# Rows of Wo freed of their mean, and the output projection of an attention layer spread over three slots

## The reference, cut to what matters

```python
x = x + _layernorm(_L0_attn_ref(_layernorm(x), Wqvk, Wo))     # x: (8, 1024, 512) f32
x = x + _layernorm(_L0_ffn_ref(_layernorm(x), W1, b1, ..., W2, b2))

def _layernorm(x, axis=-1, eps=1e-05):
    m = jnp.mean(x, axis=axis, keepdims=True)
    v = jnp.var(x, axis=axis, keepdims=True)
    return (x - m) / jnp.sqrt(v + eps)

def _L0_attn_ref(h, Wqvk, Wo):            # 16 heads of 32, causal
    ...
    wv = jnp.einsum('bsth,bthi->bshi', weights, v).reshape(b, s, d)
    return wv @ Wo
```

## Time and profile before

| | |
|---|---|
| median of three runs | 3590.53 us |
| profiled execution, whole | 3584.82 us |
| its span, first to last instruction | 3582.9 us |
| mean granted clock of TensorE | 0.956 of full |
| TensorE busy, matmuls | 3246.1 us (91%) |
| VectorE, ScalarE, POOL busy | 2240.6, 2105.8, 1333.6 us |

### The profile page before, as it was taken

How to read it: one execution, slowest core, us unless ns; L and a number is a source line. 1 busy time by engine, 2 the same in 40 slices (tenths; PEclk the granted TensorE clock), 3 DMA queues, 4 the chain that set the end, 5 groups by cost and what they waited for, 6 DMA issues and landing times. The chain is left out here.

```text
span 3582.9 us, 78215 instructions
## 1 busy us (share of the span) xinstructions
PE 3246.1 (91%) x29997; PEld 1878.0 (52%) x29997; DVE 2240.6 (63%) x4221; ACT 2105.8 (59%) x2516; POOL 1333.6 (37%) x766
## 2 busy tenths in 40 slices
PE   6999996989888889889898845999999999999998
PEld 2444442666666666667676722444444444444443
DVE  5444444777676777667676536666666666666665
ACT  2222221988888887979797924445445445445543
POOL 0000001888888897979797920000000000000000
PEclk9999996999999999999999967999999999999999
DMA  3344324122222222222213031000000000000000
GB/s 128 116 134 136 129 102 113 51 66 73 62 85 62 76 70 77 58 85 60 81 56 90 28 111 52 24 24 24 24 23 23 23 23 23 23 23 23 24 24 24
DMA packets 183098, 219.97 MB, mean 61 GB/s; under 512 B 15184, under 2 KB 129936, under 8 KB 182288
## 3 DMA queue, kind: packets, MB, share of 16 engines
q1 hardware_dynamic: 182800, 215.83, 19.1%
HBM read 130.84 MB, written 84.41 MB: 60 GB/s over the span
## 5 line engine op out<-in xcount | busy, mean ns | idle before, releaser
L949 POOL TENSOR_TENSOR a_prob_lo<-a_prob,a_prob_hi 128x2048 f16<-128x2048 f32 (+2 forms) x448 | 1192.1, 2689 | 249.9 <-ACT a_prob_hi L840 247.9
L870 DVE TENSOR_REDUCE a_mx<-a_pw 128x1 f32<-128x512 f32 (+3 forms) x1216 | 753.3, 657 | 165.7 <-PE a_pw L717 122.4
L830 ACT ACTIVATE a_prob<-a_pst,a_lift,a_exp_scale 128x1024 f32<-128x1024 f32 (+1 forms) x640 | 707.3, 1121 | 185.1 <-PE a_pst L770 97.6
L1387 PE MATMUL f_py<-f_w,f_act 128*128 128x512 f16 x3072 | 706.6, 380 | 20.2 <-DVE f_work L1153 12.8
L1377 PE MATMUL f_ph<-f_xT,f_w 128*128 128x512 f16 x3072 | 707.3, 380 | 0.0
L840 ACT ACTIVATE a_prob_hi<-a_prob 128x2048 f16<-128x2048 f32 (+2 forms) x448 | 582.7, 1301 | 0.0
L1325 ACT ACTIVATE f_hidden_work<-f_ph,f_turn,f_fold 128x512 f32<-128x512 f32 x256 | 199.0, 777 | 596.4 <-PE f_ph L1377 595.7
L712 PE MATMUL a_pw<-a_kp,a_qp 96*128 96x512 f16 (+3 forms) x1536 | 469.6, 342 | 75.0 <-DVE a_mx L870 58.4
L1108 POOL TENSOR_TENSOR f_ve<-f_mv,f_eps 128x4 f32<-128x4 f32 x32 | 9.0, 282 | 1384.5 <-DVE f_mv L1134 1384.5
L792 PE MATMUL a_acc<-a_vt,a_prob_hi 128*128 128x33 f16 x9216 | 468.4, 179 | 44.7 <-POOL a_prob_lo L949 24.4
L792 PEld LDWEIGHTS a_acc<-a_vt,a_prob_hi 128*128 128x128 f16 x9216 | 435.9, 97 | 125.3 <-DVE a_o L889 27.9
(11 more groups left out here) (170 smaller groups left out, 3526.0 us busy)
## 6 DMA issues: line engine op xcount, KB each, us to landing
qk_parts<-q_stage SPq DMA_DIRECT2D x128, 256.0 KB, 2.1
a_qp<-qk_parts SPq DMA_DIRECT2D x192, 128.0 KB, 2.6
a_kp<-qk_parts SPq DMA_DIRECT2D x192, 128.0 KB, 2.8
v_parts<-q_vstage SPq DMA_DIRECT2D x16, 1056.0 KB, 5.1
a_vt<-v_parts SPq DMA_DIRECT2D x32, 528.0 KB, 4.4
q_x<-in_L_attn_h_dram SPq DMA_DIRECT2D x16, 1024.0 KB, 7.7
a_xr<-in_L_attn_h_dram SPq DMA_DIRECT2D x64, 256.0 KB, 2.9
x<-a_y SPq DMA_DIRECT2D x64, 256.0 KB, 2.1
```

The costliest lines, as they stand in the source:

```text
L830: act.activation(prob[:, k % PR, :, off:QC], pst[:, k % 2, :, off:QC], ACT.Exp, scale=exp_scale[:, :], bias=lift[:, :]).then_inc(exp_done, 1)
L870: dve.tensor_reduce(out, src, AX_X, ALU.max).then_inc(released, 1)
L949: pool.tensor_tensor(prob_lo[:, first % HR:first % HR + steps, :, off:QC], prob[:, first % PR:first % PR + steps, :, off:QC], prob_hi[:, f ...
L1387: last = pe.matmul(py[:, t, :], act_r[:, f % AR, b, t * P:(t + 1) * P], w2s[:, a, f, :], start=(f == 0 and j == 0), stop=(f == NF - 1 and ...
```

## The change

Once, in the setup, VectorE takes the mean of each of Wo's 512 rows and subtracts it. Each row of wv @ Wo then has mean zero, its variance is what it was, and x + layernorm becomes one operation, pwo*rstd + x. ScalarE's shift and POOL's third small operation are gone. The scale is found from the subtracted rows. A tile's twelve matmuls stand in three slots, four in each. The statistics move to the end of slot 3, behind that slot's reduces, and POOL's two small operations to slot 3; y stays at the end of slot 4, in front of the statistics if two tiles met there.

```diff
-WO_STATS, WO_SMALL, WO_NORM, WO_OUT, WO_STORE = 2, 2, 3, 4, 5
+WO_PARTS = 3
+WO_STATS, WO_SMALL, WO_OUT, WO_STORE = 3, 3, 4, 5
...
                 for k in range(KT):
                     dve.wait_ge(w_loaded[k], 16)
-                    then(dve.tensor_reduce(amax[:, k:k + 1], raw[:, k, :], AX_X, ALU.max, apply_absolute_value=True))
+                    last = dve.tensor_reduce(row_mean[:, k:k + 1], raw[:, k, :], AX_X, ALU.add)
+                then(last)
+                then(dve.tensor_scalar(row_mean[:, :], row_mean[:, :], 1 / D, None, ALU.mult))
+                for k in range(KT):
+                    last = dve.tensor_scalar(raw[:, k, :], raw[:, k, :], row_mean[:, k:k + 1], None, ALU.subtract)
+                then(last)
+                for k in range(KT):
+                    last = dve.tensor_reduce(amax[:, k:k + 1], raw[:, k, :], AX_X, ALU.max, apply_absolute_value=True)
+                then(last)
...
-                    for w, a in PASSES:
-                        last = pe.matmul(pwo[:, :], oT[:, a, g, t * P:(t + 1) * P], wo[:, w, g, :],
-                                         start=(g == 0 and (w, a) == PASSES[0]),
-                                         stop=(g == GROUPS - 1 and (w, a) == PASSES[-1]))
-                    if g == GROUPS - 1:
+                    terms = [(g, a, w) for g in range(GROUPS) for w, a in PASSES]
+                    per = len(terms) // WO_PARTS
+                    for j, (g, a, w) in list(enumerate(terms))[part * per:(part + 1) * per]:
+                        last = pe.matmul(pwo[:, :], oT[:, a, g, t * P:(t + 1) * P], wo[:, w, g, :], start=(j == 0),
+                                         stop=(j == len(terms) - 1))
+                    if part == WO_PARTS - 1:
                         last.then_inc(wo_done, 1)
...
-                        for b, t in stage.tiles(u, k, WO_NORM):
-                            shift_x(i + b, t)
...
                 def wo_out(i, t):
                     s, n = t % YR, QT * i + t
-                    dve.wait_ge(x_shifted, n + 1)
+                    dve.wait_ge(small_done, 2 * n + 2)
+                    dve.wait_ge(xr_loaded[t % 2], 16 * (QT // 2 * i + t // 2 + 1))
                     wait(dve, y_stored[s], 16 * (QT // YR * i + t // YR))
                     dve.scalar_tensor_tensor(y[:, s, :], pwo[:, :], small[:, s, 1:2], xr[:, t % 2, :], ALU.mult,
-                                             ALU.subtract
+                                             ALU.add
                                              ).then_inc(y_done, 1)
...
                     for u, k in stage.slots:
-                        for b, t in stage.tiles(u, k, WO_STATS):
-                            wo_stats(i + b, t)
                         for at, what, unit, m in stage.at(u, k):
                             shared(i, at, before, what, unit, m, stage)
...
                         for b, t in stage.tiles(u, k, WO_OUT):
                             wo_out(i + b, t)
+                        for b, t in stage.tiles(u, k, WO_STATS):
+                            wo_stats(i + b, t)
...
-                    pool.wait_ge(small_done, 3 * n + 2)
-                    pool.tensor_tensor(small[:, s, 2:3], mv[:, s, 0:1], small[:, s, 1:2], ALU.mult
-                                       ).then_inc(small_done, 1)
```

More of the change, by code:

```diff
@@ L488, in attention_phase @@
         amax = sb("amax", [P, KT])
+        row_mean = sb("row_mean", [P, KT])
         top, o_pow2, o_scale, exp_scale = (sb(n, [P, 1]) for n in ("top", "o_pow2", "o_scale", "exp_scale"))
@@ L509, in attention_phase @@
         mv = sb("mv", [P, YR, 2])
-        small = sb("small", [P, YR, 3])
+        small = sb("small", [P, YR, 2])
         half = sb("half", [P, 1])
@@ L532, in attention_phase @@
         xr_loaded = [sem(f"xr_loaded{b}") for b in range(2)]
-        wo_done, x_shifted, y_done = sem("wo_done"), sem("x_shifted"), sem("y_done")
+        wo_done, y_done = sem("wo_done"), sem("y_done")
         y_stored = [sem(f"y_stored{b}") for b in range(YR)]
@@ L574, in _ @@
                 pe.wait_ge(const, 9)
-                pe.wait_ge(vec_step, KT + 1)
+                pe.wait_ge(vec_step, 5)
                 pe.transpose(pw[0:1, 0, 0:P], top[:, :], ident[:, :]).then_inc(top_turned, 1)
-                pe.wait_ge(vec_step, KT + 2)
+                pe.wait_ge(vec_step, 6)
                 pe.matmul(pw[:, 1, 0:2], ones[:, :], top_row[:, :].to_broadcast([1, 2]), start=True, stop=True
@@ L611, in _ @@
             def _(act):
-                act.wait_ge(vec_step, KT + 6)
+                act.wait_ge(vec_step, 10)
                 for k in range(KT):
@@ L739, in shared, with project @@
                     last.then_inc(work_done, 1)
-                def project(i, before, b, t, g, stage):
+                def project(i, before, b, t, part, stage):
                     n = QT * (i + b) + t
-                    if g == 0:
+                    if part == 0:
                         wait(pe, y_done, n)
-                    if g == 0 and t % TQ == 0:
+                    if part == 0 and t % TQ == 0:
                         turn = next((n for n, it in enumerate(stage.work)
@@ L814, in run @@
                                 shared(i, at, before, what, unit, m, stage)
-                        for part in range(2):
+                        for part in range(WO_PARTS):
                             for b, t in stage.tiles(u, k, part):
-                                for g in range(2 * part, 2 * part + 2):
-                                    project(i, before, b, t, g, stage)
+                                project(i, before, b, t, part, stage)
                 for at, (what, m) in enumerate(AHEAD):
@@ L841, in high @@
                                    prob[:, first % PR:first % PR + steps, :, off:QC], ACT.Copy).then_inc(hi_done, 1)
[L843 to L847, removed]
                 def run(i, stage):
@@ L958, in wo_small @@
                     pool.tensor_tensor(small[:, s, 0:1], mv[:, s, 1:2], eps[:, :], ALU.add).then_inc(small_done, 1)
-                    pool.wait_ge(small_done, 3 * n + 1)
+                    pool.wait_ge(small_done, 2 * n + 1)
                     pool.tensor_tensor(small[:, s, 1:2], small[:, s, 0:1], half[:, :], ALU.pow).then_inc(small_done, 1)
-                    pool.wait_ge(small_done, 3 * n + 2)
-                    pool.tensor_tensor(small[:, s, 2:3], mv[:, s, 0:1], small[:, s, 1:2], ALU.mult
-                                       ).then_inc(small_done, 1)
                 def run(i, stage):
```

## The result

The changed kernel took 3645.98 us (median of four runs, 3645.12 to 3652.05), the kernel before beside it 3590.98; ratio 1.0157, 95% interval 1.0139 to 1.0174. It is 55 us slower; 3630 was forecast, in a range of 3582 to 3660. The profiled execution took 3645.1 us, its span is 3643.3.

The account below looks back on a forecast made before the run. Tiles cost about 33 us a batch, mostly engines waiting for one another; ScalarE and POOL set the pace in unit 2. Terms 42.7 + 2 - 4 + 0.3 give +41 us, so 3630, range 3582 to 3660.

Parts of the forecast that it names:

- the slip: At tiles 1, 3, 5 and 7, POOL's small operations come 4.08 us later, behind one more subtraction.
- Tiles 3 and 7: Slot 5 of units 0 and 1: VectorE stands 2.4 us, slot 11's scores come late; +1.9 and +1.7 us.
- Tiles 4 and 0: Units 0 and 3, slot 10: statistics and two reduces before the last product eat the shift's gain; -0.25 and -0.7 us.
- Tiles 5 and 1: Units 0 and 3, slot 15: product slips; tiles 4 and 5 together +2.5 us, tile 1's 2.3 us mostly hidden.
- Rival (a), the clock: After TensorE's longer stops (tiles 3, 5, 7) it runs at 1.2 GHz; 34 us on top, 3662; chance 0.15.
- Rival (b): At slots 13 to 14 and 18 to 19 the shift held the loop; removal makes it faster, 3552; chance 0.14.
- Rival (c), hidden: Two pw banks and score buffers cover the slip at tiles 3 and 7; only drain and setup left, 3587; chance 0.09.
- Drain: Six tiles alone after the last batch: shorter chain between them, -4 us; TensorE stops 2.75 instead of 3.77 us.
- Setup: Before the loop: row means added, VectorE's setup moves from 588.4 to 592.6 - 593.3; +0.3 us (bounds 0 and 1.5).
- the low case of the range: With tile 7 at 0.5, tile 3 at 1.0 and tile 5 at 1.2 less, whole change +17 us.

Follow-up runs that it names:

- e2: The kernel before with only the mean-free rows of Wo, shift and POOL's third operation gone, slots and order as before: 3529.84 us.
- e1: The changed kernel with POOL's two small operations ahead of slot 3's subtraction instead of behind it: 3523.52 us.
- e9: The kernel before, shift kept, with POOL's three small operations ahead of its subtraction and one slot earlier: 3521.94 us.
- e5: e2 with POOL's two small operations ahead of its subtraction and one slot earlier: 3509.45 us.
- e3: The changed kernel with POOL's small operations ahead of slot 3's subtraction at tiles 3 and 7 alone: 3592.86 us, one run.
- e8: The changed kernel with POOL's small operations ahead of slot 3's subtraction at tiles 1, 3 and 7 alone: 3555.19 us, one run.
- e6: e2 with a ScalarE operation of the shift's size put back in slot 3 of each tile, its result unused: 3527.31 us.

## Why the prediction was right, point by point

The sign, the place and the size came out (+41 on the profiled execution forecast, +60.3 measured), and the mechanism holds: y at tiles 1, 3, 5 and 7 waits for POOL's small operations behind one more subtraction, and hardly at the others. But that the sum came so near is in part luck: it hit by two terms that were too small with opposite signs. e2 and e1 show them apart, taken one after the other: the removal of the shift gives 61 us, the new slots with POOL in time 6 (e2 to e1), and the slip takes 122, which is +55; where the working had about 2.4 us of slip a tile and counted of the shift only "what the late engine gets of it". The size of a term depends on this order: with POOL in time already (e9 to e5) the shift's removal gives 12.5.

| per batch (1 to 6), from scores to scores, us | predicted | measured |
|---|---|---|
| tile 3 (slots 10 to 13 of unit 0) | +1.9 | +4.6 |
| tile 7 (slots 10 to 13 of unit 1) | +1.7 | +4.4 |
| tiles 4 and 5 (slots 14 to 19, and 0 to 9 of unit 1) | +2.5 | -2.1 + 2.9 = +0.8 |
| tiles 0 and 1 (slots 10 to 19 of unit 3, and 0 to 9 of unit 0) | -0.5 | -3.3 + 3.8 = +0.5 |
| the other stretches | 0 | -0.9 |
| sum | +5.6 | +9.5 |

- **Tiles 3 and 7: mis-sized.** VectorE stood 3.43 us and not 2.4: the 0.9 us by which ScalarE's high part was to come earlier did not show. And the scores of slot 11 come not 0.9 us behind y, with their first half; exponential 11 needs both halves, and between them TensorE makes a piece for the maxima. By the rows above, the exponential now starts 2.3 us after the first of the four matmuls and waits 3.51 us for them; before, it started 2.2 us after the first of six (1184.01 to 1186.18 in the earlier trace rows) and waited for nothing. What four instead of six saves is given back, and the granted clock is half there. From 1208.5 on, and again behind tile 7's stop:

```profile
1208.50:1211.50 3.00, 3.00 (x28) 2.05 (x27) 1.95 (x5) 1.56 (x2) 2.35 (x1) 0.53 0.54 175
1266.70:1270.10 3.40, 3.40 (x40) 2.34 (x38) 2.77 (x7) 2.61 (x3) 3.39 (x2) 0.50 0.47 154
```

- **Tiles 4 and 0: the step that failed.** The prediction let the statistics and two reduces in front of y eat the shift's gain and took -0.25 and -0.7 us. y at tile 4 has no wait at all, and the stretches are 2.1 and 3.3 us shorter. The wait for the shift, 1.51 us in the earlier trace rows, was there to be read as a gain. VectorE at tile 4 of the changed kernel, with no wait in front:

```profile
1219.53 0.75 DVE L917 SCALAR_TENSOR_TENSOR a_y<-a_pwo,a_small,a_xr 128x512 f32<-128x512 f32 x1
```

- **Tiles 5 and 1: mechanism right, a term missing.** Unit 0 was to grow to about 56 us and has 57.2; unit 1 was to have about 47 and has 54.0. Tile 5's stop (VectorE 6.20, TensorE 5.71) falls into unit 1, where the working had booked it in unit 0, and tile 1's falls into unit 0. Tile 1 was said to vanish beside TensorE's turn of 3.92 us. It did not: VectorE has a turn of its own, 3.1 us from branch to next instruction, that comes behind y and ended behind TensorE's already, and e3 and e8 put 4.7 us on each tile 1.
- **Rival (a), the clock: no.** Over batches 1 to 6 TensorE is idle 174.8 us instead of 120.5, 54 us of the 57; its busy time rises only from 988.6 to 991.0, and of that 98.0 us are at half clock, where it was 105.9. The new stops bring half clock, and those that went took theirs along. In a kernel with shorter stops the clock then gives something: e2 has 103.8 us of idle time and 968.2 of busy time with the same matmuls, so 17 of its 37 us in those batches are idle time and 20 are busy time; 50.8 us of its busy time are at half clock, where before it was 105.9.
- **Rival (b): its result was real, its reason was not.** The prediction held against it that POOL takes its subtractions back to back, so a freer ScalarE does not bring them forward. True, and beside the point: y waits for the shift, which stands behind POOL, and gets the 1.0 us whether or not POOL moves. At tiles 0 and 4 of the changed kernel this gain is there as well. The Trainium skill (Perfetto Trace Analysis, Identifying the Most-Contended Engine) would have the fullest engine relieved first. No run here tries that rule on ScalarE: it is the fullest in unit 2 alone (37.24 of 38.50 us), which held no shift, and in units 3, 0 and 1 TensorE is busier than it by the earlier trace rows. What e6 does show is that the 46 us which the working let come back by that rule do not come from ScalarE's busy time.
- **Rival (c), hidden: no.** TensorE's two banks covered next to nothing of a 3.43 us wait: it stopped for 3.19.
- **Drain: right.** What follows the last exponential is 4.1 us shorter, against 4. TensorE's stop between two tiles is the 2.75 us named, against 3.77 in the earlier trace rows:

```profile
2169.06 0.75 DVE L917 SCALAR_TENSOR_TENSOR a_y<-a_pwo,a_small,a_xr 128x512 f32<-128x512 f32 x1 [0.93 <-POOL a_small L963]
...
2169.86 4.03 PE L763 MATMUL a_pwo<-a_wo,a_oT 128*128 128x512 f16 x12 [2.75 <-DVE a_y L917]
```

- **Setup: right, near nothing.** VectorE's setup ends at 591.94 us, 0.7 before the earliest end worked out (592.6), and the first exponential starts at 626.87 instead of 627.34. Two of VectorE's rows of it, the means and the subtractions:

```profile
579.96 0.98 DVE L598 TENSOR_SCALAR a_row_mean<-a_row_mean 128x4 f32<-128x4 f32 x1
580.98 1.77 DVE L600 TENSOR_SCALAR a_raw<-a_raw,a_row_mean 128x512 f32<-128x512 f32 x4
```

- **Slips of the working.** The tiles of a batch cost 31.7 us by the earlier trace rows and not about 33 (49.75 + 51.85 + 45.60 less three times 38.50), rival (a)'s sum is 3664 and not 3662, and the low case of the range comes to +18 and not +17. None of them moves the forecast.

## What to carry to other kernels

A small operation that others wait for should stand, on an engine that executes in order, ahead of the long one that it need not follow, where the engine idles anyway. POOL's 0.8 us of small work behind a 4 us subtraction set the time of units in which POOL was never full, and moving it gave 66 us, where taking the shift out gave 61 before the move and 12.5 behind it. Before an operation is taken out or moved, read its wait and who is released by it; the busy time removed says little (45.6 us on a ScalarE that was not full: nothing). An edit that is slower as a whole (by 55 us) may hold a gain as large (61 us): test the parts apart. Two effects of 60 and 120 us can sum to a forecast that looks right.

## What the runs showed of the hardware that was not expected

- VectorE stands 2.54 us where its loop turns ("issue" in the row above), TensorE 3.92 at its own. The Trainium skill (Runtime: NRT & Kernel Launch, Instruction fetch mechanics) says that a taken branch whose target is outside the fetched window waits for a fetch. Both stops stand at the loop's branch, which agrees: VectorE's branch record is followed by nothing for 3.1 us, while POOL, which has the fewest instructions in a pass (146 records against VectorE's 502), loses 0.3 us at the same branch. But no run here took the branch away.
- The scaling of 128x4 row sums took 0.98 us, where tiny operations of VectorE's setup take 0.15 to 0.16 us each. POOL's memset, of 3.51 us, ends in the same moment:

```profile
577.41 3.51 POOL L639 MEMSET a_kp<- 2x4096 f16 x1
```

The Trainium skill (SBUF — State Buffer, Who interferes with whom) has it that of a VectorE operation in a two-port mode and a POOL instruction the one that comes second is blocked until the first ends; the row agrees (579.96 + 0.98 = 580.94, memset to 580.92), on this one instance. The next one points the same way: while VectorE's four subtractions ran (580.98 to 582.75), POOL's three mask operations took 0.55, 0.47 and 0.46 us, where each took 0.29 in the kernel before. In which mode VectorE ran is not shown.
